# A depthwise 5x5 convolution on TensorE: from 25 square tiles of 121 pixels to 24 oblong tiles of 126

## The reference

```
y = lax.conv_general_dilated(x, k, window_strides=(1, 1), padding='SAME',
        dimension_numbers=('NHWC', 'HWIO', 'NHWC'), feature_group_count=ch)
return x + y
```

## Time and profile before

| | |
|---|---|
| time, median of 3 (lowest, highest) | 827.06 us (826.73, 827.2) |
| the profiled execution: its time, its span | 826.83 us, 825.0 us |
| PE, PEld busy | 99%, 99% of the span, 7200 each |
| DVE, ACT, POOL busy | 81%, 75%, 72% |
| HBM read, written | 158.55 MB, 149.42 MB: 373 GB/s over the span |

### The profile page before, as it was taken

The page is one execution under the profiler, slowest core; times in us unless marked ns, Lnnn a source line. Parts: engine busy times, 40 slices in busy tenths (PEclk is TensorE's granted clock), DMA queues, the critical chain, the costliest instruction groups (busy, mean ns, idle before and its releaser), DMA issues.

```text
span 825.0 us, 20812 instructions
## 1 busy us (share of the span) xinstructions
PE 814.7 (99%) x7200; PEld 814.5 (99%) x7200; DVE 670.8 (81%) x2118; ACT 619.6 (75%) x1538; POOL 591.9 (72%) x389
## 2 busy tenths in 40 slices
PE   6999999999999999999999999999999999999998
PEld 6999999999999999999999999999999999999998
DVE  6888888878788887878888888878888887888886
ACT  5777777777777777777777777777777777777775
POOL 6768577696775867858668677685775867758662
PEclk9999999999999999999999999999999999999999
DMA  9999999999999999999999999999999999999975
GB/s 364 414 388 402 354 395 375 376 381 367 402 371 376 384 371 395 376 368 400 355 382 398 368 400 363 373 397 356 401 372 378 353 404 384 377 365 405 363 317 227
DMA packets 28759, 309.29 MB, mean 375 GB/s; under 512 B 3184, under 2 KB 3312, under 8 KB 4208
## 3 DMA queue, kind: packets, MB, share of 16 engines
q1 hardware_dynamic: 28656, 307.98, 97.1%
HBM read 158.55 MB, written 149.42 MB: 373 GB/s over the span
## 4 chain that ended last, share of the span: by engine, by line
PE 99%; POOL 0%; DMA 0%; issue 0%; ACT 0%; DVE 0%; DVEq 0%
PE sums L419 66%; PE sums L415 33%; POOL matrix L237 0%; DMA first<-consts 0%; POOL expanded L228 0%; POOL taps L219 0%; POOL spare L216 0%; POOL taps L214 0%; ACT y_out L307 0%; DVE y_out L357 0%; DVEq L95 0%
## 5 line engine op out<-in xcount | busy, mean ns | idle before, releaser
L419 PE MATMUL sums<-matrix,x_high 121*128 121x240 f32 (+3 forms) x4800 | 814.2, 278 | 0.0
L419 PEld LDWEIGHTS sums<-matrix,x_high 121*128 121x128 f32 x4800 | 730.7, 192 | 0.0
L415 PE MATMUL sums<-matrix,x_low 121*128 121x240 f32 (+3 forms) x2400 | 665.8, 277 | 6.8 <-POOL matrix L237 6.8
L307 ACT ACTIVATE y_out<-sums 128x220 f32<-128x220 f32 (+6 forms) x1248 | 420.5, 376 | 194.3 <-PE sums L419 175.8
L357 DVE TENSOR_TENSOR y_out<-sums,y_out 128x60 f32<-128x60 f32 (+5 forms) x1824 | 358.8, 227 | 144.6 <-ACT y_out L307 62.6
L415 PEld LDWEIGHTS sums<-matrix,x_low 121*128 121x128 f32 x2400 | 460.4, 192 | 6.9 <-POOL matrix L237 6.8
L265 POOL TENSOR_TENSOR x_low<-x_in,x_high 121x640 fp32r<-121x640 f32 x190 | 320.7, 1710 | 119.0 <-DVE x_high L331 119.0
L340 DVE TENSOR_TENSOR x_low<-x_in,x_high 121x1280 fp32r<-121x1280 f32 (+1 forms) x194 | 290.2, 1497 | 2.2 <-ACT x_high L297 2.1
L297 ACT ACTIVATE x_high<-x_in 121x640 fp32r<-121x640 f32 (+1 forms) x288 | 263.6, 916 | 7.3 <-DMA x_in<-x 7.3
L253 POOL TENSOR_TENSOR matrix<-expanded,mask 121x600 fp32r<-121x600 f32 x95 | 157.9, 1662 | 92.4 <-PE sums L419 90.5
L331 DVE CAST x_high<-x_in 121x640 fp32r<-121x640 f32 x96 | 68.1, 710 | 3.8 <-DMA x_in<-x 3.3
(11 more groups left out here) (5 smaller groups left out, 0.6 us busy)
## 6 DMA issues: line engine op xcount, KB each, us to landing
x_in<-x SPq DMA_DIRECT2D x95, 1600.0 KB, 10.2
y<-y_out SPq DMA_DIRECT2D x95, 1520.0 KB, 13.2
rest<-later SPq DMA_DIRECT2D x1, 1150.0 KB, 12.1
x_in<-x SPq DMA_DIRECT2D x3, 320.0 KB, 3.6
y<-y_out SPq DMA_DIRECT2D x1, 852.5 KB, 3.6
x_in<-x SPq DMA_DIRECT2D x1, 640.0 KB, 6.1
y<-y_out SPq DMA_DIRECT2D x1, 365.0 KB, 2.3
y<-y_out SPq DMA_DIRECT2D x1, 302.5 KB, 2.7
```

The costliest lines, as they stand in the source:

```text
L307: act.activation(outputs(c, rows, cols), sums(c, t, rows, cols), ACT.Copy).then_inc(copied, 1)
L415: pe.matmul(target, x_low[c % SLOTS][0:PIXELS, at:at + IMAGES], window(c, strip, k, slice(HIGH, HIGH + 1)).squeeze(1), start=k == tile["sq ...
L419: product = pe.matmul(target, x_high[c % SLOTS][0:PIXELS, at:at + IMAGES], window(c, strip, k, slice(part, part + 1)).squeeze(1), start=Fa ...
```

## The change

The plane is cut into 24 tiles of 9x14 pixels instead of 25 of 11x11. Twelve tiles lie flat (9 rows by 14 columns) and twelve are tall (14 by 9), in four quarters that turn around the middle pixel: flat at the top left, tall at the top right, flat at the bottom right, tall at the bottom left. The middle pixel, which no tile covers, is the 127th row of tile 5. Two tiles side by side along their long side make one bank: 12 banks, 6 matmuls each, 72 in a channel. Each has 11, 13 or 14 rows of 16 or 18 columns. Over a channel the moving columns are 3 x 5066 = 15198, where they were 3 x 5396 = 16188.

A tall tile is laid out turned: its pixels are numbered with the long side as the inner one, and its matrix is built from turned taps, so that PE sees the same shapes, and the sums lie turned in PSUM with a pitch of 30. ACT and DVE then read them with the inner index stepping by 30 elements, and write `y_out` upright. Six of the 12 copies (1375 of 3025 elements) and nine of the 14 adds (845 of 1445 elements; before, 19 adds had 1344) read so.

Other parts: all `x_low` pieces are now made by DVE (four pieces of 768 columns), none by POOL. POOL makes two matrices for each channel, flat and tall, each in two halves of 300 cells, from two copies of 200 elements for each channel; the taps it splits are twice as many (200 elements for four channels). The mask is loaded by a DMA instead of being computed. The loads of x are 128 rows of 12288 B at a pitch of 12416 B, where they were 12800 B without gaps; the constants are larger (125 KB for 80 KB, and 2300 KB for 1150 KB later). The last channel is stored in two parts instead of three: rows 0 to 24 after the sixth bank, the rest (832.5 KB) at the end.

```diff
-SQUARE = 11
-ACROSS = SIDE // SQUARE
-PIXELS = SQUARE * SQUARE
-IN_COLS = ACROSS * ACROSS * IMAGES
-STRIP_COLS = ACROSS * IMAGES
+LONG, SHORT = 14, 9
+PIXELS = LONG * SHORT
+CENTRE = SIDE // 2
+FLAT, TALL = range(2)
+KINDS = 2
+
+QUARTERS = (
+    (FLAT, (0, 14), (0, 9, 18)),
+    (TALL, (0, 14), (28, 37, 46)),
+    (FLAT, (27, 41), (28, 37, 46)),
+    (TALL, (27, 41), (0, 9, 18)),
+)
+PER_BANK, PER_QUARTER = 2, 6
+TILE_COUNT = len(QUARTERS) * PER_QUARTER
+CENTRE_TILE = 5
+IN_COLS = TILE_COUNT * IMAGES
+IN_PITCH = IN_COLS + 32
+PIECE_COLS = PER_QUARTER * IMAGES
+PIECES = len(QUARTERS)
...
-REACH = SQUARE + 2 * HALO
-ROW = 4 * TAPS
-MATRIX = REACH * ROW
 FILTER = TAPS * TAPS
-EXPANDED = TAPS * ROW
+ROWS, COLS = 15, 20
+CELLS = ROWS * COLS
 HIGH, LOW = range(2)
...
+HIGH_AFTER = (2, 5, 7)
+CAST_AFTER = 2
+LOW_AFTER = (4, 5, 7, 9)
...
+def banks_of_plane():
+    banks = []
+    for quarter, (kind, along, across) in enumerate(QUARTERS):
+        for n, v in enumerate(across):
+            deep = SHORT + (quarter == 0 and n == len(across) - 1)
+            short, long = reach(v, deep), (reach(along[0], LONG)[0], reach(along[-1], LONG)[1])
+            rows, cols = (short, long) if kind == FLAT else (long, short)
+            tiles = []
+            for k, u in enumerate(along):
+                a, b = reach(u, LONG)
+                tiles.append(dict(
+                    at=(quarter * PER_QUARTER + n * PER_BANK + k) * IMAGES,
+                    pixels=PIXELS + (quarter * PER_QUARTER + n * PER_BANK + k == CENTRE_TILE),
+                    deep=short[1] - short[0], wide=(a - long[0], b - long[0]),
+                    from_row=short[0] - (v - HALO), from_col=a - (u - HALO)))
+            banks.append(dict(quarter=quarter, kind=kind, rows=rows, cols=cols, tiles=tiles,
+                              deep=short[1] - short[0], pitch=long[1] - long[0]))
+    return banks
+
...
+def plan_of_sums(banks):
+
+    covered = np.zeros((SIDE, SIDE), bool)
+    earlier = []
+    for bank in banks:
+        cells = np.zeros((SIDE, SIDE), bool)
+        cells[slice(*bank["rows"]), slice(*bank["cols"])] = True
+        (bank["copy"],) = rectangles(cells & ~covered)
+        seams = sorted(rectangles(cells & covered), key=lambda r: (r[0][0] < r[0][1] and (
+            [n for n, e in enumerate(earlier) if meet(e, r)] or [-1])[-1]))
+        bank["adds"] = []
+        for seam in seams:
+            after = [n + 1 for n, e in enumerate(earlier) if meet(e, seam)]
+            bank["adds"].append((seam, after[-1] if after else 0))
+            earlier.append(seam)
+        covered |= cells
+    return len(earlier)
+
...
+        def plane_of(c, t):
+            bank = PLAN[t]
+            return psum[:, (c * BANK_COUNT + t) % BANKS, 0:bank["deep"] * bank["pitch"]].rearrange(
+                "p (v u) -> p v u", u=bank["pitch"])
 
...
+            top, left = PLAN[t]["rows"][0], PLAN[t]["cols"][0]
+            plane = plane_of(c, t)
+            if PLAN[t]["kind"] == TALL:
+                plane = plane.rearrange("p x y -> p y x")
+            return plane[:, rows[0] - top:rows[1] - top, cols[0] - left:cols[1] - left]
...
-                sp.dma_start(x_in[c % X_SLOTS][:, :], x[c, :, :]).then_inc(x_loaded[c % X_SLOTS], 16)
+                    sp.wait_ge(low_ready, PIECES * (c - X_SLOTS + 1))
+                sp.dma_start(x_in[c % X_SLOTS][:, :], x[c, :, 0:IN_COLS]).then_inc(x_loaded[c % X_SLOTS], 16)
...
                 sp.dma_start(x_in[0][:, cols], x[0, :, cols]).then_inc(loaded, 16)
+                if piece == 0:
+                    sp.dma_start(mask[:, :, :], masks[:, :, :]).then_inc(masks_loaded, 16)
...
             c = CHANNELS - 1
-            for a, b in LAST_STORES:
-                sp.wait_ge(added, ADDS * c + ADDS_BEFORE[strip_tiles(b - 1)[-1] + 1])
-                done = SIDE * start_of(a)
-                end = SIDE * start_of(b) if b < ACROSS else OUT_COLS
+            split = SIDE * TOP_ROWS
+            for t, done, end in ((TOP_BANKS, 0, split), (BANK_COUNT, split, OUT_COLS)):
+                sp.wait_ge(added, ADDS * c + ADDS_BEFORE[t])
                 sp.dma_start(out[c, :, done:end], y_out[c % Y_SLOTS][:, done:end]).then_inc(y_stored[c % Y_SLOTS], 16)
...
+            def spread_taps(c):
+                if c:
+                    pool.wait_ge(matrix_step, 2 * KINDS * c)
+                for kind in range(KINDS):
+                    shape = [whole, 2 * TAPS, COLS // TAPS, TAPS]
+                    rows = taps[0:whole, c % GROUP, kind, :, :].bitcast(F32).rearrange("p h (d e) -> p (h d) e", e=TAPS)
+                    pool.tensor_copy(
+                        spread[kind][0:whole, :, :].rearrange("p h (d a e) -> p (h d) a e", d=TAPS, e=TAPS),
+                        rows.unsqueeze(2).broadcast_to(shape)).then_inc(spread_step, 1)
...
             def make_matrix(c):
+                pool.wait_ge(spread_step, KINDS * (c + 1))
+                if c == 0:
...
+                    pool.wait_ge(sums_done, BANK_COUNT * (c - SLOTS + 1))
+                for kind in range(KINDS):
+                    shape = [whole, ROWS // TAPS, TAPS * COLS]
+                    for part in (HIGH, LOW):
+                        pool.tensor_tensor(
+                            matrix[c % SLOTS][kind][0:whole, part, :].rearrange("p (b e) -> p b e", b=ROWS // TAPS),
+                            spread[kind][0:whole, part, :].unsqueeze(1).broadcast_to(shape),
+                            mask[0:whole, kind, :].rearrange("p (b e) -> p b e", b=ROWS // TAPS),
+                            ALU.mult).then_inc(matrix_step, 1)
+
+            for c in range(CHANNELS):
                 if c % GROUP == 0:
                     split_taps(c // GROUP)
-                    pool.wait_ge(matrix_step, c + 1)
-                    spread_taps((0, GROUP))
-                    pool.wait_ge(spread, c // GROUP + 2)
+                spread_taps(c)
                 make_matrix(c)
...
+            def copy_bank(c, t):
+                act.wait_ge(sums_done, BANK_COUNT * c + t + 1)
+                if t == 0 and c >= Y_SLOTS:
+                    act.wait_ge(y_stored[c % Y_SLOTS], 16 * (c // Y_SLOTS))
+                rows, cols = PLAN[t]["copy"]
+                act.activation(outputs(c, rows, cols), sums(c, t, rows, cols), ACT.Copy).then_inc(copied, 1)
...
+            def add_seams(c, t):
+                for n, ((rows, cols), after) in enumerate(PLAN[t]["adds"]):
+                    if n == 0:
+                        dve.wait_ge(copied, BANK_COUNT * c + t + 1)
+                    if after:
+                        dve.wait_ge(added, ADDS * c + after)
+                    y = outputs(c, rows, cols)
+                    dve.tensor_tensor(y, sums(c, t, rows, cols), y, ALU.add).then_inc(added, 1)
...
+                for t in range(BANK_COUNT):
+                    add_seams(c, t)
+                    if c + 1 < CHANNELS:
+                        if t == CAST_AFTER:
+                            cast_high(c + 1)
+                        if t in LOW_AFTER:
+                            split_low(c + 1, LOW_AFTER.index(t))
...
+                for t, bank in enumerate(PLAN):
+                    kind, quarter = bank["kind"], bank["quarter"]
+                    if t % (BANK_COUNT // PIECES) == 0:
+                        if quarter < KINDS:
+                            pe.wait_ge(matrix_step, 2 * KINDS * c + 2 * (kind + 1))
+                        pe.wait_ge(low_ready, PIECES * c + quarter + 1)
...
+                    for tile in bank["tiles"]:
+                        deep, wide, pixels = tile["deep"], tile["wide"], tile["pixels"]
+                        target = plane_of(c, t)[:, 0:deep, slice(*wide)]
+                        images = slice(tile["at"], tile["at"] + IMAGES)
+                        high, low = x_high[c % SLOTS][0:pixels, images], x_low[c % SLOTS][0:pixels, images]
+                        turned = [matrix[c % SLOTS][kind][0:pixels, part, :].rearrange("p (r q) -> p r q", q=COLS)[
+                            :, tile["from_row"]:tile["from_row"] + deep,
+                            tile["from_col"]:tile["from_col"] + wide[1] - wide[0]] for part in (HIGH, LOW)]
+                        last = tile is bank["tiles"][-1]
+                        pe.matmul(target, low, turned[HIGH], start=tile is bank["tiles"][0], stop=False,
+                                  skip_group_check=True)
+                        pe.matmul(target, high, turned[LOW], start=False, stop=False, skip_group_check=True)
+                        product = pe.matmul(target, high, turned[HIGH], start=False, stop=last, skip_group_check=True)
                     product.then_inc(sums_done, 1)
```

More of the change, by code:

```diff
@@ L95, in build, with meet @@
+def meet(a, b):
+    return all(p[0] < q[1] and q[0] < p[1] for p, q in zip(a, b))
+PLAN = banks_of_plane()
+ADDS = plan_of_sums(PLAN)
+BANK_COUNT = len(PLAN)
+ADDS_BEFORE = [sum(len(b["adds"]) for b in PLAN[:n]) for n in range(BANK_COUNT + 1)]
```

(5 more changed lines are left out.)

322 lines of the change are left out of this document (93 added, 229 removed).

## The result

| | before | after |
|---|---|---|
| median (lowest, highest; runs) | 827.13 us (826.73, 827.42; 4) | 821.13 us (820.37, 822.11; 4) |
| span of the profiled execution | 825.0 us | 818.6 us |
| matmuls, and one of them between 60 and 800 us | 7200, 0.1127 us | 6912, 740/6369 = 0.1162 us |

The change gains 6.0 us, a ratio of 0.9928 with the interval [0.9911, 0.9946]. I had forecast 29.8. At the pace of before, 6.0 us is the time of 53 matmuls (6.0/0.1127), and 288 are gone.

The account below looks back on a forecast made before the run. PE bounds the kernel, each matmul costing its weight load. Span 825.0 - 32.5 (matmuls) + 1.2 (start) + 1.6 (end) = 795.3; with 1.8 around it 797.1, median 0.2 higher: 797.3 us, range 792 to 804 (788 to 824 with rivals).

Parts of the forecast that it names:

- The pace: PE's matmuls: 288 fewer, each still 0.1127 us whatever its shape; 32.5 us gained.
- Time goes by the matmul, not by the column, up to 240: PE in mid-run: 208 columns cost no less than 240, so fewer columns gain nothing.
- The bound on this term: PE's matmuls: if 252 and 234 columns cost 5 ns more each, 24 a channel, +11.5 us.
- if the pace depends on rows 18 wide: Sign that the forecast is wrong, in PE's matmul pace; given no size.
- The floor: PE: each matmul costs the load of 128 weight columns before it, 107 ns by the skill, 112.7 in the trace.
- Start and end: Start: POOL's longer chain before the first matmul, +1.2 us (0.7 to 1.6). End: larger last store and one more add, +1.6.
- Pixels: PE's matmuls: contracting over 126 pixels instead of 121 costs nothing; 32 us if time went by pixels.
- DVE: the mechanism: DVE needs 7.9 us a channel (7.3 to 9.3), inside PE's 8.11; rival that DVE or exclusion bounds: 818 us, 9 in 100.
- Turned reading: Rival at DVE's PSUM reads: elements at inner step 30 cost k times as much; put at 845 us, 11 in 100.
- DMA was not the bound: DMA needs 386 GB/s, cost 0; rival that 378 GB/s is all it gives: 813 us, 9 in 100.
- POOL: POOL's work takes about 5 us a channel, 1 to 2 more with blocking, inside 8.11; cost 0.
- Columns set the pace: Rival for PE's matmuls: time goes by moving columns, 50 us gained instead of 32.5; about 780 us, 5 in 100.

Follow-up runs that it names:

- experiment 5: The kernel before, with its windows that began at column 0 of the matrix grid moved to column 2 (other sums); 893.96 us in one run.
- the probes: Two runs of the changed kernel with blocks of 24 equal matmuls behind its last add, to measure single shapes; 320 columns in one run took 0.147 us each.
- experiment 2: The changed kernel with each moving operand read as one run without gaps, same sizes and PSUM side (other sums); 791.58 us in one run.
- experiment 1: The changed kernel with every matmul contracting over 121 pixels instead of 126 or 127; 820.26 us in one run.
- compact kernel: The changed kernel with matrix rows at a pitch of 18 instead of 20, same sums; 792.68 us median of 5 runs, 0.9583 of the kernel before.

## Why the prediction was wrong, point by point

**The pace: this step failed.** The prediction said "Three matmuls with 252 columns exceed what rows show; at 2.4 GHz 252 columns stream in 105 ns, still under 112.7", and took 0.1127 us for all 6912. The runs showed that streaming does not go by columns. A row of the window costs some 4.4 cycles for each group of 4 columns, rounded up, and one more group if its width is a multiple of 4 and its start is not; a matmul takes the larger of that sum and a floor of 0.112 us. With this rule a channel of the changed kernel comes out as:

- 9 matmuls of 13 rows of 16 from column 2: 13 x 5 x 4.4 = 286 cycles, 0.119 us each, so 0.065 us above the floor in all;
- 21 of 13 rows of 18: 286 cycles too, 0.151 us;
- 3 of 14 rows of 16 from column 2, and 3 of 14 of 18: 308 cycles, 0.128 us, 0.098 us;
- the other 36 at the floor.

72 x 0.112 + 0.314 = 8.38 us; the trace has 72 x 0.1162 = 8.37. For the pitch of 18 the same count gives 8.08 and the trace 8.07. For the kernel before it gives 0.1126 us a matmul (0.1127 measured), and for experiment 5 0.1229 (0.1221). The rule's numbers come from the probes and the floor from experiment 2, so these sums are a cross-check. 0.314 x 96 = 30 us, almost the 32.5 that 288 matmuls give, go into the 36 matmuls of each channel that left the floor. The kernel before, at 0.1127, had paid 5 us of this kind (7200 x 0.0007). That leaves 25 us, where 24 were measured.

**"Time goes by the matmul, not by the column, up to 240" was read from too few rows.** I compared the 240 columns at 404.66 with the 208 at 405.65. Both read from column 0, and both stood at the floor: 15 rows of 16 are 15 x 17.6 = 264 cycles = 0.110 us, just below 0.112. The next row of that group, 208 columns at 405.99, was the clue. It reads from column 1, 13 x 22 = 286 cycles, and takes 0.35/3 = 0.117 up to the next square's start:

```profile
406.34 0.27 PE L415 MATMUL sums<-matrix,x_low 121*128 121x208 f32 x1
```

That is fewer columns than 240, and slower. I had listed the row and not taken its pace. The kernel before stood within 2% of both limits, and experiment 5 shows how near: off column 0 the same instructions cost 67 us more.

**The bound on this term** was 5 ns for 24 matmuls a channel, +11.5 us. It had the 18 wide rows, and missed the 12 matmuls of rows of 16 from column 2, and the size (7 to 16 ns and not 5). Added to the forecast it gives 808.8 us, so the range, which ended at 804, was narrower than this one bound; the measured 821.13 lies outside both. The last sentence of the prediction, that it is wrong "if the pace depends on rows 18 wide", named half of it without a price; a price from below (rows cost nothing) and from above (each row costs a fixed extra) would have widened the range for the right reason.

**The floor was right.** "What each matmul costs is the load of 128 weight columns before it" holds for half of the matmuls: 0.112 for 64 columns (L405, (817.15 - 814.80)/21, the part of the block in this view), as for 176 to 208. With 64 weight columns it falls to 0.059 at the same clock (L407), so it does go by the weight columns.

**Start and end.** The first matmul is at 8.25 us where 8.0 was expected, and 6.84 before: +1.4, with 1.2 taken. POOL's timeline there, after the constants: 

```profile
2.94 0.57 POOL L236 TENSOR_TENSOR taps<-first 127x200 fp32r<-127x200 f32 x1 [2.50 <-DMA first<-consts]
...
4.94 1.58 POOL L250 COPY spread<-taps 127x200 f32<-127x200 f32 x2
6.60 3.88 POOL L263 TENSOR_TENSOR matrix<-spread,mask 127x300 fp32r<-127x300 f32 x4
```

The two copies take 1.58 together, where I allowed 1.2 at most. The last store, 832.5 KB, landed in 3.4 us, and the end took 1.3 us more than before where 1.6 was taken. **Pixels** were rightly put at nothing: with 121 of them the pace stayed at 0.1161 (experiment 1).

**DVE: the mechanism was right, the size 0.7 us too large.** Its groups by shape, beside the earlier trace rows:

```profile
L323 DVE TENSOR_TENSOR x_low<-x_in,x_high 128x768 fp32r<-128x768 f32 x384 | 379.8, 989 | 2.0 <-ACT x_high L285 2.0
L333 DVE TENSOR_TENSOR y_out<-sums,y_out 128x120 f32<-128x120 f32 x768 | 202.3, 276 | 116.6 <-ACT y_out L292 112.6
```

A low of 768 takes 0.989 us in the mean, where 0.87 alone and below 1.3 were expected. DVE is busy 690.1/96 = 7.2 us a channel where I took 7.9: as PE's channel was longer as well (8.37), DVE was never close. In the compact kernel it was inside 8.07 too.

**Turned reading costs nothing.** The 768 adds of 120 elements are both kinds. Taken apart by the bank they read, the upright ones take 0.275 us and the turned ones, whose inner step in PSUM is 30 elements, 0.277. k is 1.0. The Trainium skill (SBUF — State Buffer, section Door 1) has PSUM lines of 8 bytes, and says that non-contiguous patterns slow matmuls; I had carried this over to readers as k = 2. The trace does not agree, neither for readers (0.277) nor for PE's writes in rows of 16 with gaps between them (a block of 3.68 us against 3.69).

**DMA was not the bound.** Between 12 and 60 us it moved 426 GB/s, and in the compact kernel 385 all along, at the same share of 0.99 that the earlier trace rows has for 378. The share said only that a packet was open, as read.

**POOL** took 525.6/96 = 5.5 us a channel, where about 5 and 1 to 2 of blocking were expected, and PE never waited for it again. **Columns set the pace,** as put, was wrong: the kernel would have been faster than forecast. The columns rival and the forecast shared the error that a column's price is the same in any row.

## What to carry to other kernels

Before a tiling is judged by its number of matmuls, work out both limits for each shape: the floor per matmul and the stream of its moving window, the latter by row, with widths rounded up to 4 and starts looked at; a shape whose window is one run, or whose rows are a multiple of 4 wide and begin at one, is the cheap one. When two shapes of different size run at one pace, that does not say that size is free: they may stand at two limits that happen to be equal, and the shape that is slow for its size (here 208 columns at 0.117) shows the second one. A few blocks of 24 equal matmuls at the end of a kernel measure such a thing better than any mean of the kernel.
